# One product on constants ahead of the taps' product in a vision tower, and key weights issued by ScalarE

## The chip, the cores and the metric

The kernel runs on one core of a Trainium2 chip. TensorE multiplies matrices, VectorE, ScalarE and GpSimd do the rest, and SyncE (SP) issues most of the transfers between memory (HBM) and the core's SBUF. The number to compare is the device time of one execution in microseconds (us). Before the change it is 248.19 us, the median of 3 runs (247.21 to 248.34).

## The reference

Eight pictures of 3 x 256 x 256 go through an edge filter, one causal attention head, a layer norm, a mixture of 8 experts with a capacity, and a second layer norm.

```python
# x (8, 3, 256, 256); scharr (2, 1, 3, 3): the taps; D = 256, 8 experts, F = 1024
gray = einsum('bchw,c->bhw', x, (0.2989, 0.587, 0.114))
h = sum over both filters of |conv3x3(gray, scharr)| / 2          # (8, 256, 256): 256 tokens of 256
Q, K, V = h @ Wq.T + bq, h @ Wk.T + bk, h @ Wv.T + bv
h = layernorm(h + softmax(causal(Q @ K.T / 16)) @ V)
probs = softmax(h @ Wr);  idx = argmax(probs)                     # each token goes to one expert
kept = position within its expert < 320
ffn = where(kept, (relu(t @ W1[idx]) @ W2[idx]) * max(probs), t)
out = layernorm(h + ffn)
```

## The kernel before, in words

The program is written by engine: a block for each of SyncE, GpSimd, ScalarE, VectorE and TensorE, each run in the order in which it stands, with semaphores between them. There is no planner: the order is written out by hand. Most products are done in three parts on fp32r halves ("high" and "low" of a number), the setup products in fp32, which the trace shows as two passes each.

The stages are: a setup; then a loop over the 8 pictures, which interleaves the convolution of the next picture (`convolve`, as products with band matrices) with the attention of the present one; then a loop over 8 experts. TensorE goes from one to the next with hardly a break. The change touches the setup alone, the first 10 us:

- SyncE issues the taps (18 numbers), Wq, Wk, the top and the bottom half of the first picture, Wv, Wr, the second picture and the biases of the values (lines 369 to 380).
- VectorE sets `one_row` (a row of ones, line 917) and fills one quarter of `xT_hi` with ones (line 918; the trace calls this memory `w_hi`). Then it scales the spread taps (`half_taps`, 920) and builds the three bands (`make_band`, lines 900 and 908), with two parts of them from ScalarE, and then the first picture's gray values (927 to 934, the trace's `red`).
- ScalarE issues the key bias (749, into the last column of `wk`), copies the row of ones (752, which brings a table load), makes parts of the bands (758), issues the query bias (760), rounds the bands (636, `band_high`) and then the gray values (764, 766).
- TensorE spreads the taps over 128 partitions with a product of `one_row` and `taps` (1463). Behind it come six products on the ones (`keep_warm`, 1458), whose result no one reads; they fill the time in which the weights of the keys are under way. Then `setup_keys` multiplies Wq and Wk (1302; it waits for both, `attn_w_in` at 32, and for the key bias, `key_bias_in`), `setup_biases` makes the bias terms (1311, 1314; waits for the query bias), and the convolution of the first picture begins (1364; waits for the bands and the high half of the gray values, `first_gray_ready`).

Of the kernel before, what the change touches and what calls it, by code (L numbers as in the profile page):

```python
# [10 lines left out]
F32 = mybir.dt.float32  # L11
# [21 lines left out]
def vit_tower_kernel(  # L33
# [13 lines left out]
):  # L47
    B, CH, S, D = x.shape
    E, _, F = W1.shape
    DC, SC, FC = D // P, S // P, F // P  # L50
    T = B * S
# [15 lines left out]
    with ExitStack() as ctx:  # L67
        def sb(name, shape, dt=F32):
            return ctx.enter_context(nc.sbuf_tensor(name, shape, dt))

        def sem(name):
            return ctx.enter_context(nc.semaphore(name))
# [22 lines left out]
        wk = sb("wk", [P, DC, D + 1])  # L95
# [22 lines left out]
        def halves(start, *dims):  # L118
            n = int(np.prod(dims))
            names = "abc"[:len(dims)]  # L120
            cut = f"p ({' '.join(names)}) -> p {' '.join(names)}"
            sizes = dict(zip(names, dims))
            return [t[:, start:start + n].rearrange(cut, **sizes) for t in (attn_hi, attn_lo)]

        xT_hi, xT_lo = halves(0, 2, DC, S)
# [124 lines left out]
        attn_w_in = sem("attn_w_in")  # L250
        wv_in = sem("wv_in")
        still_ready = sem("still_ready")
# [80 lines left out]
        def _(sp):  # L333
# [34 lines left out]

            sp.dma_start(taps[:, :], bass.AP(scharr.tensor, 0, [[0, 1], [1, TAP_COLS]])).then_inc(taps_in, 16)
            sp.dma_start(wq[:, :, :], Wq.rearrange("(p c) d -> p c d", c=DC)).then_inc(attn_w_in, 16)  # L370
            sp.dma_start(wk[:, :, 0:D], Wk.rearrange("(p c) d -> p c d", c=DC)).then_inc(attn_w_in, 16)
            sp.dma_start(pix[:, 0, :, 0, :], x[0, :, 0:P, :].rearrange("c p d -> p c d")).then_inc(first_pix, 16)
            sp.dma_start(pix[:, 0, :, 1, :], x[0, :, P:S, :].rearrange("c p d -> p c d")).then_inc(pix_in[0], 16)
            sp.dma_start(wv[:, :, :], Wv.rearrange("(c p) d -> p c d", p=P)).then_inc(wv_in, 16)
# [247 lines left out]
        def _(act):  # L622
# [117 lines left out]
            def split_high(n):  # L740
# [4 lines left out]
                if e >= 2:  # L745
                    act.wait_ge(h_used, FC * (e - 1))
                act.activation(w_hi[:, e % 2, c], w_raw[:, e % 2, c], ACT.Copy).then_inc(w_hi_ready, 1)  # L747

            act.dma_start(wk[:, :, D:D + 1], bk.rearrange("(p c o) -> p c o", c=DC, o=1),
                          allow_slow_non_contiguous=True).then_inc(key_bias_in, 16)  # L750
            act.wait_ge(row_ready, 1)
# [82 lines left out]
            def norm_out(e):  # L834
                act.wait_ge(yrstd_ready, e + 1)
                if e >= 2:
                    act.wait_ge(z_out[e % 2], 16 * NS * (e // 2))
                for j, (_, n) in enumerate(SLOTS):
                    ins = act.activation(z[0:n, e % 2, j, :], y[0:n, e % 2, j, :], ACT.Identity,  # L839
                                         bias=ynmr[0:n, e % 2, j:j + 1], scale=yrstd[0:n, e % 2, j:j + 1])  # L840
                ins.then_inc(z_ready, 1)
# [22 lines left out]
        def _(dve):  # L864
# [6 lines left out]
            def settle():  # L871
                dve.wait_ge(dve_step, steps[0])
# [23 lines left out]
            def make_band(dx):  # L896
# [8 lines left out]
                for dy in range(1, TAPS):  # L905
# [8 lines left out]
                    if dy < TAPS - 1:  # L914
                        settle()

            dve.memset(one_row[:, :], 1.0).then_inc(row_ready, 1)
            dve.memset(xT_hi[:, 0].bitcast(F32), 1.0).then_inc(still_ready, 1)
            dve.wait_ge(taps_spread, 1)
            dve.tensor_scalar(half_taps[:, :], bank[4][:, 0:TAP_COLS], 0.5 * GRAY[0], None, ALU.mult).then_inc(scaled_ready, 1)  # L920
            dve.wait_ge(mask_ready, TAPS)
# [291 lines left out]
            def expert_out(e):  # L1213

                if e >= 2:
                    dve.wait_ge(z_ready, e - 1)
                dve.wait_ge(turned, e + 1)
                if e == 0:
                    dve.wait_ge(ein_in[0], 64)
                for j, (_, n) in enumerate(SLOTS):  # L1220
                    at, o = TURNED[j]
                    dve.scalar_tensor_tensor(y[0:n, e % 2, j, :], bank[at][0:n, o:o + D],
                                             ein[0:n, e, j, D:D + 1], ein[0:n, e, j, 0:D],
                                             ALU.mult, ALU.add).then_inc(y_ready, 1)

            def expert_stats(e):
                for j, (_, n) in enumerate(SLOTS):
                    dve.wait_ge(y_ready, NS * e + j + 1)
                    step(dve.bn_stats(ystats[0:n, j, :], y[0:n, e % 2, j, :]))
# [58 lines left out]
        def _(pe):  # L1288
# [8 lines left out]
            def setup_keys():  # L1297
                pe.wait_ge(attn_w_in, 16 * 2)
                pe.wait_ge(key_bias_in, 16)
                for c, to in enumerate((bank[3], bank[6])):  # L1300
                    for k in range(DC):
                        ins = pe.matmul(to[:, 0:D + 1], wq[:, k, c * P:(c + 1) * P],  # L1302
                                        wk[:, k, :], start=(k == 0), stop=(k == DC - 1))
                ins.then_inc(setup_mm, 1)
# [151 lines left out]
            def keep_warm(n):  # L1456
                for _ in range(n):
                    pe.matmul(bank[3][:, :], xT_hi[:, 0, 0, 0:P], xT_hi[:, 0].rearrange("p c s -> p (c s)"),  # L1458
                              start=True, stop=True)

            pe.wait_ge(row_ready, 1)
            pe.wait_ge(taps_in, 16)
            pe.matmul(bank[4][:, 0:TAP_COLS], one_row[:, :], taps[:, :], start=True, stop=True).then_inc(taps_spread, 1)
            pe.wait_ge(still_ready, 1)
            keep_warm(6)
            setup_keys()
            setup_biases()
            for s in range(SC):
# [58 lines left out]
            def early_turn():  # L1527
                pe.wait_ge(rowc_ready, B)
                pe.wait_ge(ein_in[0], 32)
                pe.wait_ge(spare_rows_ready, 1)  # L1530
                for c in range(DC):
                    for j, (o, _) in enumerate(SLOTS):
                        ins = pe.matmul(bank[c][:, o:o + P], ein[:, 0, j, c * P:(c + 1) * P], ident[:, :],
                                        start=(j == 0), stop=False, is_transpose=True, skip_group_check=True)
                ins.then_inc(early_turned, 1)
# [125 lines left out]
```

## Time and profile before

| | us |
|---|---|
| median of 3 runs | 248.19 (247.21 to 248.34) |
| the profiled execution | 248.55 |
| its span, first to last instruction | 246.7 |
| TensorE busy | 231.8 (94%) |
| VectorE busy | 185.3 (75%) |
| ScalarE busy | 152.1 (62%) |
| GpSimd busy | 99.4 (40%) |

The profile is of one execution. Its span leaves out 1.85 us that the time holds. Times in rows count from the start of the span. PE is TensorE's products, PEld its loading of weights, DVE VectorE, ACT ScalarE, POOL GpSimd; SPq and ACTq are the sequencers of SyncE and ScalarE when they issue transfers. The end of a product is modelled, since products overlap in the array: the step from one start to the next tells its rate better than its own duration does. L12 is line 12 of the kernel.

### The profile page before, as it was taken

To read this page: it belongs to the slowest core of one execution; us is meant where nothing else is said; L and a number is where in the kernel's file an instruction comes from. 1 tells how busy PE (TensorE), PEld (TensorE's weight loads), DVE (VectorE), ACT (ScalarE), POOL (GpSimd) and SP (SyncE) were. 2 spreads that over 40 slices of the span, in tenths; PEclk is the share of its full clock that TensorE was granted. 3 is DMA by queue.
4 is the path that set the end of the run, shared out by engine and by line. 5 is a ranking of instruction groups with operands and counts; after the bars stand their busy time and mean duration, and the time that the engine had idled before them with its cause. 6 is when DMAs were issued, how large, how long until landed. Compare 5 with 4: busy or idle time off the path is not lost.

```text
span 246.7 us, 4992 instructions
## 1 busy us (share of the span) xinstructions
PE 231.8 (94%) x1670; PEld 222.6 (90%) x1670; DVE 185.3 (75%) x559; ACT 152.1 (62%) x355; POOL 99.4 (40%) x169
## 2 busy tenths in 40 slices
PE   6999999999999999878999999999999999999940
PEld 4999999999999998656999999999999999999940
DVE  6868797888878798976666787867878678789550
ACT  5337567786877787465675676575765757666100
POOL 7000227484655669448100025133261322613672
PEclk9999999999999999999999999999999999999995
DMA  5925994174796020201799929156091550100100
GB/s 163 286 87 137 254 297 140 35 230 154 231 383 231 12 82 3 84 0 48 182 348 303 372 45 332 53 172 205 5 339 53 173 200 3 47 0 24 35 4 0
DMA packets 28379, 35.48 MB, mean 144 GB/s; under 512 B 2781, under 2 KB 25292, under 8 KB 28355
## 3 DMA queue, kind: packets, MB, share of 16 engines
q1 hardware_dynamic: 26146, 31.71, 40.8%
q0 software_dynamic: 1792, 3.47, 3.9%
q8 instruction: 13, 0.21, 0.4%
q14 instruction: 12, 0.09, 0.1%
q10 hardware_dynamic: 416, 0.00, 0.1%
HBM read 26.97 MB, written 9.47 MB: 148 GB/s over the span
## 4 chain that ended last, share of the span: by engine, by line
PE 82%; issue 5%; DVE 4%; POOL 4%; ACT 2%; POOLq 1%; DMA 0%; DVEq 0%; ACTq 0%
PE bank L1293 15%; PE bank L1294 15%; PE bank L1295 15%; PE bank L1364 12%; PE bank L1381 5%; PE bank L1418 4%; POOL out_dram L575 3%; PE bank L1547 2%; PE bank L1434 2%; PE bank L1597 2%; PE bank L1392 1%; PE bank L1302 1%; PE bank L1436 1%; PE bank L1435 1%; PE bank L1458 1%
## 5 line engine op out<-in xcount | busy, mean ns | idle before, releaser
L1210 DVE SCALAR_TENSOR_TENSOR h_lo<-bank,h_hi 128x320 fp32r<-128x320 f32 x58 | 28.4, 490 | 26.8 <-ACT h_hi L822 24.0
L822 ACT ACTIVATE h_hi<-bank 128x320 fp32r<-128x320 f32 x58 | 25.4, 438 | 36.8 <-PE bank L1295 36.8
L1293 PE MATMUL bank<-einT_hi,w_hi 128*128 128x320 f32 x128 | 40.4, 316 | 0.5 <-DVE einT_lo L1202 0.3
L1295 PE MATMUL bank<-einT_hi,w_lo 128*128 128x320 f32 x128 | 39.6, 309 | 0.0
L575 POOL DMA_INDIRECT out_dram<-tokens_mem,images x24 | 27.8, 1157 | 29.3 <-ACT tokens_mem L839 22.2
L1294 PE MATMUL bank<-einT_lo,w_hi 128*128 128x320 f32 x128 | 39.5, 309 | 0.0
L959 DVE TENSOR_TENSOR w_lo<-w_raw,w_hi 128x1024 fp32r<-128x1024 f32 x32 | 38.9, 1215 | 0.0
L1293 PE MATMUL bank<-h_hi,w_hi 128*128 128x320 f32 x112 | 35.2, 315 | 0.1
L1294 PE MATMUL bank<-h_lo,w_hi 128*128 128x320 f32 x112 | 34.6, 309 | 0.0
L1295 PE MATMUL bank<-h_hi,w_lo 128*128 128x320 f32 x112 | 34.6, 309 | 0.0
L747 ACT ACTIVATE w_hi<-w_raw 128x1024 fp32r<-128x1024 f32 x32 | 33.7, 1053 | 0.0
L569 POOL TENSOR_TENSOR yrstd<-yve,minus_half 128x3 f32<-128x3 f32 x6 | 5.3, 880 | 55.1 <-DVE yve L1241 55.1
L1293 PEld LDWEIGHTS bank<-einT_hi,w_hi 128*128 128x128 f32 x128 | 24.0, 188 | 1.6 <-issue 1.0
L1294 PEld LDWEIGHTS bank<-einT_lo,w_hi 128*128 128x128 f32 x128 | 24.1, 188 | 0.0
L1295 PEld LDWEIGHTS bank<-einT_hi,w_lo 128*128 128x128 f32 x128 | 24.0, 188 | 0.0
L1293 PEld LDWEIGHTS bank<-h_hi,w_hi 128*128 128x128 f32 x112 | 21.1, 188 | 0.3 <-issue 0.3
L1294 PEld LDWEIGHTS bank<-h_lo,w_hi 128*128 128x128 f32 x112 | 21.1, 188 | 0.0
L1295 PEld LDWEIGHTS bank<-h_hi,w_lo 128*128 128x128 f32 x112 | 21.0, 188 | 0.0
L525 POOL DMA_INDIRECT dispatched<-trow,slot x16 | 16.4, 1026 | 7.3 <-issue 5.7
L1364 PE MATMUL bank<-w_hi 128*128 128x260 f32 x96 | 15.1, 292 | 0.0
L1293 PE MATMUL bank<-w_hi 128*128 128x274 f32 (+2 forms) x50 | 14.5, 291 | 0.4 <-DVE w_lo L1210 0.4
L1364 PE MATMUL bank<-w_lo,w_hi 128*128 128x260 f32 x96 | 14.8, 291 | 0.0
(232 smaller groups left out, 575.4 us busy)
## 6 DMA issues: line engine op xcount, KB each, us to landing
w_raw<-in_L_ffn_W_dram SPq DMA_DIRECT2D x16, 1024.0 KB
images<-in_x_dram SPq DMA_DIRECT2D x7, 768.0 KB
dispatched<-blank SPq DMA_DIRECT2D x4, 645.0 KB, 10.0
images<-dispatched SPq DMA_DIRECT2D x9, 258.0 KB, 5.9
out_dram<-lone SPq DMA_DIRECT2D x8, 256.0 KB, 6.9
images<-in_x_dram SPq DMA_DIRECT2D x2, 384.0 KB, 4.5
images<-dispatched SPq DMA_DIRECT2D x9, 64.5 KB, 7.1
out_dram<-tokens_mem,images POOLq DMA_INDIRECT x24
```

The lines of the kernel that those rows point to most:

```text
L525: pool.indirect_dma_start(dispatched, bass.IndirectOffsetOnAxis(ap=slot[:, b % TR, s:s + 1], axis=0), trow[:, b % TR, s, :], None, bounds_ ...
L575: pool.indirect_dma_start(out_rows, bass.IndirectOffsetOnAxis(ap=ein[0:n, e, j, D + 1:D + 2].bitcast(U32), axis=0), z[0:n, e % 2, j, :], N ...
L747: act.activation(w_hi[:, e % 2, c], w_raw[:, e % 2, c], ACT.Copy).then_inc(w_hi_ready, 1)
L822: act.activation(hidden_halves(n)[0], bank[n % 2][:, 0:CAP], ACT.Relu).then_inc(h_hi_ready, 1)
L959: dve.tensor_tensor(w_lo[:, e % 2, c], w_raw[:, e % 2, c], w_hi[:, e % 2, c].bitcast(F32), ALU.subtract).then_inc(w_lo_ready, 1)
L1210: dve.scalar_tensor_tensor(lo, bank[n % 2][:, 0:CAP], 0.0, hi.bitcast(F32), ALU.max, ALU.subtract).then_inc(h_ready, 1)
L1293: pe.matmul(to, ah, bh, start=first, stop=False)
L1294: pe.matmul(to, ah, bl, start=False, stop=False)
L1295: return pe.matmul(to, al, bh, start=False, stop=last)
L1364: ins = pe.matmul(acc[:, :, s * (S - REACH):s * (S - REACH) + REACH], half[:, b % 2, s, c * P + dx:c * P + dx + P], of_band[:, dx, :, 2 - ...
L1381: ins = pe.matmul(bank[3][:, c * S:(c + 1) * S], half[:, k, c * P:(c + 1) * P], of_x[:, b % 2, k, :], start=(t == c == k == 0), stop=(t == ...
L1418: ins = pe.matmul(bank[6][:, s * S:s * S + n], half[:, k, s * P:(s + 1) * P], of_x[:, b % 2, k, 0:n], start=(t == s == k == 0), stop=(t == ...
```

## The change

TensorE does one of the products on constants before the product that spreads the taps, and five behind it. For that VectorE fills the ones first and sets the row of ones second. Wk is issued by ScalarE's queue, ahead of the key bias, and no longer by SyncE's.

```diff
@@ -368,7 +368,6 @@
             sp.dma_start(taps[:, :], bass.AP(scharr.tensor, 0, [[0, 1], [1, TAP_COLS]])).then_inc(taps_in, 16)
             sp.dma_start(wq[:, :, :], Wq.rearrange("(p c) d -> p c d", c=DC)).then_inc(attn_w_in, 16)
-            sp.dma_start(wk[:, :, 0:D], Wk.rearrange("(p c) d -> p c d", c=DC)).then_inc(attn_w_in, 16)
             sp.dma_start(pix[:, 0, :, 0, :], x[0, :, 0:P, :].rearrange("c p d -> p c d")).then_inc(first_pix, 16)
@@ -746,6 +745,7 @@
+            act.dma_start(wk[:, :, 0:D], Wk.rearrange("(p c) d -> p c d", c=DC)).then_inc(attn_w_in, 16)
             act.dma_start(wk[:, :, D:D + 1], bk.rearrange("(p c o) -> p c o", c=DC, o=1),
                           allow_slow_non_contiguous=True).then_inc(key_bias_in, 16)
             act.wait_ge(row_ready, 1)
@@ -914,8 +914,8 @@
+            dve.memset(xT_hi[:, 0].bitcast(F32), 1.0).then_inc(still_ready, 1)
             dve.memset(one_row[:, :], 1.0).then_inc(row_ready, 1)
-            dve.memset(xT_hi[:, 0].bitcast(F32), 1.0).then_inc(still_ready, 1)
             dve.wait_ge(taps_spread, 1)
@@ -1458,11 +1458,12 @@
+            pe.wait_ge(still_ready, 1)
+            keep_warm(1)
             pe.wait_ge(row_ready, 1)
             pe.wait_ge(taps_in, 16)
             pe.matmul(bank[4][:, 0:TAP_COLS], one_row[:, :], taps[:, :], start=True, stop=True).then_inc(taps_spread, 1)
-            pe.wait_ge(still_ready, 1)
-            keep_warm(6)
+            keep_warm(5)
             setup_keys()
```

TensorE's order at the start of the program, before and then after; `one_row` and `taps` are the taps' product, `w_hi` the ones:

```order
L1287 UNCONDITIONAL_BRANCH
L1463 MATMUL bank<-taps,one_row 128x18
L1458 MATMUL bank<-w_hi 128x512 x6
L1302 MATMUL bank<-wk,wq 128x257 x4
L1311 MATMUL bank<-bqc,wk 128x1 x4
L1314 MATMUL bank<-wk,bqc 128x1 x2
```

```order
L1287 UNCONDITIONAL_BRANCH
L1458 MATMUL bank<-w_hi 128x512
L1465 MATMUL bank<-taps,one_row 128x18
L1458 MATMUL bank<-w_hi 128x512 x5
L1302 MATMUL bank<-wk,wq 128x257 x4
L1311 MATMUL bank<-bqc,wk 128x1 x4
```

One of the six products stands ahead of the taps' product; the rest of TensorE's order is as it was.

SyncE's transfers at the start, the piece of the difference (- before, + after); `images` is the picture:

```order
 L369 DMA taps<-in_L_tok_scharr_dram 1x18
 L370 DMA wq<-in_L_attn_Wq_dram 128x512
-L371 DMA wk<-in_L_attn_Wk_dram 128x2x256
+L371 DMA images<-in_x_dram 128x3x256
 L372 DMA images<-in_x_dram 128x3x256
-L373 DMA images<-in_x_dram 128x3x256
-L374 DMA wv<-in_L_attn_Wv_dram 128x2x256
-L375 DMA wr<-in_L_ffn_Wr_dram 128x2x8
+L373 DMA wv<-in_L_attn_Wv_dram 128x2x256
+L374 DMA wr<-in_L_ffn_Wr_dram 128x2x8
```

Everything behind Wq moves up by one place in SyncE's queue. ScalarE's start, the other end of that move, after the change:

```order
L748 DMA wk<-in_L_attn_Wk_dram 128x2x256
L749 DMA wk<-in_L_attn_bk_dram 128x2x1
L752 ACT_TABLE_LOAD
L752 ACTIVATE still_row<-one_row 1x128
L758 ACTIVATE images<-images,half_taps 128x132 x4
L760 DMA bqc<-in_L_attn_bq_dram 128x2
```

Before, the same rows stood there without the first.

## Rows read from the trace of the kernel before

**Rows 1.** The page: shares of the chain that ended last, by engine

```profile
PE 82%; issue 5%; DVE 4%; POOL 4%; ACT 2%; POOLq 1%; DMA 0%; DVEq 0%; ACTq 0%
```

**Rows 2.** Waits of TensorE, whole span: total us, times, longest us

```profile
PE bank L1463 <- DMA taps<-in_L_tok_scharr_dram: 2.1, 1, 2.1
```

**Rows 3.** The chain in order of time: start us, us, what

```profile
0.80 1.21 DMA taps<-in_L_tok_scharr_dram
...
2.72 2.86 PE bank L1458 x6
```

**Rows 4.** TensorE, narrow stretches, and its weight load: start us, us, line, operation

```profile
2.65 0.80 PE L1458 MATMUL bank<-w_hi 128*128 128x512 f32 x1
...
4.95 0.63 PE L1458 MATMUL bank<-w_hi 128*128 128x512 f32 x1
5.38 0.76 PE L1302 MATMUL bank<-wk,wq 128*128 128x257 f32 x1
...
5.34 3.07 PEld L1302 LDWEIGHTS bank<-wk,wq 128*128 128x128 f32 x8 [0.48 <-DMA wk<-in_L_attn_Wk_dram]
...
8.07 0.60 PE L1302 MATMUL bank<-wk,wq 128*128 128x257 f32 x1
8.50 0.39 PE L1302 MATMUL bank<-wk,wq 128*128 128x257 f32 x1
8.72 0.28 PE L1311 MATMUL bank<-bqc,wk 128*128 128x1 f32 x2
```

**Rows 5.** Busy time by stretch; at the end granted clock, DMA share, GB/s

```profile
2.00:3.00 1.00, 0.86 (x3) 0.85 (x4) 0.18 (x1) 0.99 (x3) 0.80 (x9) 1.00 0.09 7
3.00:4.00 1.00, 1.00 (x3) 0.81 (x3) 0.92 (x4) 1.00 (x5) 0.94 (x5) 1.00 0.93 321
```

**Rows 6.** VectorE in order of time, 0 to 9 us

```profile
0.88 0.17 DVE L917 MEMSET one_row<- 1x128 f32 x1 [0.88 <-PEq L1648]
1.10 0.48 DVE L918 MEMSET w_hi<- 128x512 f32 x1
...
7.34 0.42 DVE L927 SCALAR_TENSOR_TENSOR red<-images 128x256 f32<-128x256 f32 x1
...
8.78 0.43 DVE L932 SCALAR_TENSOR_TENSOR red<-images 128x256 f32<-128x256 f32 x1 [0.56 <-DMA images<-in_x_dram]
```

**Rows 7.** Issues and ScalarE in order of time, 0 to 6 us

```profile
0.81 0.64 ACTq L749 DMA_DIRECT2D wk<-in_L_attn_bk_dram  x1
...
1.21 0.37 SPq L370 DMA_DIRECT2D wq<-in_L_attn_Wq_dram  x1
...
1.48 1.28 ACT L752 ACT_TABLE_LOAD   x1 [1.48 <-PEq L1648]
1.62 0.67 SPq L371 DMA_DIRECT2D wk<-in_L_attn_Wk_dram  x1
...
2.98 0.40 ACTq L760 DMA_DIRECT2D bqc<-in_L_attn_bq_dram  x1
2.99 1.28 ACT L758 ACTIVATE images<-images,half_taps 128x132 f32<-128x132 f32 x4
...
5.04 0.42 ACT L636 ACTIVATE w_hi<-images 128x264 fp32r<-128x264 f32 x1 [0.78 <-DVE images L908]
```

**Rows 8.** Transfers issued up to 24 us: KB each, median us to landing

```profile
wq<-in_L_attn_Wq_dram SPq DMA_DIRECT2D x1, 256.0 KB, 3.4
wk<-in_L_attn_Wk_dram SPq DMA_DIRECT2D x1, 256.0 KB, 3.7
...
wk<-in_L_attn_bk_dram ACTq DMA_DIRECT2D x1, 1.0 KB, 3.2
bqc<-in_L_attn_bq_dram ACTq DMA_DIRECT2D x1, 1.0 KB, 4.7
```

**Rows 9.** ScalarE's first gray values and TensorE's first convolution, in order of time

```profile
8.26 0.42 ACT L764 ACTIVATE w_hi<-red 128x256 fp32r<-128x256 f32 x1 [0.37 <-DVE red L929]
...
9.98 0.97 PE L1364 MATMUL bank<-w_hi 128*128 128x260 f32 x6
```

## The prediction

> **What bounds the kernel now.** I read the page's busy shares and its chain's shares first, to see whether the start of the program matters at all. TensorE is busy for 94% of the span (the table) and carries 82% of the chain that ended last [rows 1]. So time taken away ahead of TensorE's first useful product moves the whole program, unless something later waits for a thing that doesn't move with it. The list of TensorE's waits says that nothing of the kind is near: the longest of the whole span is 2.1 us, for the taps at the start [rows 2], and no other transfer stands in it.
>
> Then I read the chain in order of time. It begins with the taps' transfer, runs through the taps' product and the six products on constants [rows 3] and on into the key product; TensorE's own instructions follow.
>
> Third came TensorE's single products at the start [rows 4]. The reader is to see start-to-start times: the products on constants (512 columns) follow each other at 0.43 us, the passes of the key product (257 columns, two passes for each fp32 product) at 0.43 us too, up to the one at 8.07. The one that starts at 8.50 gives way after 0.22 us. The granted clock is printed as 1.00 in these stretches [rows 5], but 512 columns in 0.43 us are the level of 1.2 GHz, and half of the time for the same pass is that of 2.4 GHz. So in this execution the clock rises at 8.5 us, 5.85 us after the first product on constants began; up to there each microsecond of TensorE's time does half of what it does later. That is the price used below: **whatever only moves work inside the low stretch is worth half its length.**
>
> Last, what feeds this stretch: VectorE's rows [rows 6], the issues on the two queues [rows 7] and the time from an issue to landing [rows 8].
>
> **The change, part by part.**
>
> *The first product on constants goes ahead of the taps.* Its data is the memset of 0.48 us, now first on VectorE. VectorE is free at 0.88 [rows 6], so it is done at 1.36. With 0.1 us for the handover (an estimate: TensorE began at 2.14, 0.13 us after the 2.01 at which the taps' piece of the chain ends [rows 3]) the product starts near 1.47 and gives way 0.43 us later, near 1.9 to 2.0. TensorE sat idle there until 2.14. The taps' product is queued behind it: if the taps come at 2.14 as before, the margin is 0.15 us. Should it miss them, VectorE's scaling of the taps, the three bands and the picture's top rows at 7.34 are late by as much; I cost this at nothing, at most 0.2 us. The row of ones moves behind the long memset and is ready at about 1.53: ScalarE uses it only after its table load (ends 2.76), TensorE not before 2.14. Nothing is lost.
>
> *Five products in place of six behind the taps.* The first starts at 2.65 as before, the key product at 5.38 - 0.43 = 4.95. If the clock still rises at 8.50, the eight passes start from 4.95 to 8.07 and the next instruction (the bias product, at 8.72 before) at 8.50: **0.22 us gained**. Its lower end is 0, if the operands are not there at 4.95; no row makes the removed pass worth more than 0.43 us.
>
> *The clock.* TensorE now does its first wide product 1.18 us earlier (1.47 for 2.65), with a gap of about 0.2 us and the narrow taps' product behind it. Four executions of the same program took 247.21 to 248.55 us, a spread of 1.34 us, and the one with the profile is the slowest of them. At half a microsecond per microsecond of late rise, 1.34 us are 2.7 us of the clock's rise, so I read the rise at 8.50 as a late one, and the moment as not tied firmly to the program (an estimate from the spread; one trace can't show it). Then an earlier first product moves the rise by something between nothing (if the gap spoils what came before it) and the whole 1.18 us on average: 0 to 0.59 us of time. I take **0.35 us**, a bit over the middle, since the gap is short beside what is filled.
>
> The Trainium skill bears on that: "TensorE: Matmul & The Clock Gate", Part 1, What's actually happening, says that the chip's monitor of TensorE's activity runs freely and doesn't restart with the kernel, so that the moment of the rise varies between runs. The spread of the times agrees; that the rise moved in the other three executions no row shows.
>
> *Key weights from ScalarE's queue.* Before, Wk was issued at 1.62 as SP's third transfer and landed 3.7 us later, at 5.32; TensorE's weight load waited for it until 5.34 [rows 4]. It would be too late for the key product at 4.95. Now it goes out at 0.81, first on ScalarE's queue. With the same 3.7 us it lands at 4.51; Wq, issued at 1.21, at 4.61 as before [rows 7, 8]. The key bias is issued behind Wk's 0.67 us, at 1.48, and lands at 4.68 by its old 3.2 us. All three are in by 4.95, with 0.27 us to spare. The first ends of these are not sure: the bias ran at a time when the DMA engines were nearly idle (a share of 0.09 between 2 and 3 us), while from 3 us on the share is 0.93 and more [rows 5]. The query bias, a transfer of the same small kind sent at 2.98 into this traffic, took 4.7 us. With 4.7 us [rows 8] the key bias lands at 6.2. So the key product starts between 4.95 and 6.2; I take 4.95 to 5.1, as the bias still goes out before the traffic starts, and keep 6.2 for the range.
>
> ScalarE's engine waits behind one more issue: 0.67 us. Its table load moves from 1.48 to 2.15 and ends at 3.43, the copy of the row of ones at 3.7; its four band products start then in place of 2.99 and end near 5.0. ScalarE's next step waited for VectorE's first band until 5.04 [rows 7], and VectorE needs ScalarE's parts only behind that band. So it is hidden with some 0.05 us of cover. Without it the bands are late by the excess, up to 0.3 us, which stands against the slack ahead of the convolution, below.
>
> *SP's queue moves up by 0.7 us.* Picture, value weights and router weights are issued 0.7 us earlier, by Wk's issue of 0.67. VectorE had idled 0.56 us for the picture's second half at 8.78 [rows 6]; that wait goes. No one on TensorE's side gains by it now, but it is cover for a convolution that starts earlier: the first one, at 9.98, needs the high half of the picture's top rows, which ScalarE finishes at 8.26 + 0.42 = 8.68 [rows 9]. That comes from the band work on VectorE and doesn't move. So 1.3 us is the most that this part of the program can give, whatever the clock does.
>
> **The sum.** 0.22 + 0.35 = 0.57 us against the profiled execution's 248.55 (span 246.7, 1.85 us around it) would be 247.98. The median of the three timed runs stands 0.36 us under it, and a median is what I forecast: 248.19 - 0.57 = **247.6 us**. About 0.5%, 1.24 us, is what a measurement of this kernel can tell from no change.
>
> **The rivals.**
>
> *A rise one good step earlier.* If filling the time from 1.47 makes the clock rise before the key product is through, the gain isn't 0.35 us but the cap of 1.3: the key passes at 0.22 us would be done by about 7, the bias product would wait for the query bias (2.98 + 4.7 = 7.7), and the convolution would start at 8.7 for 9.98. That is 248.19 - 1.3 = 246.9. For it: the late rise in the profiled run leaves room. Against: the product ahead of the taps is short, and a gap follows it.
>
> *No effect.* The operands set the start of the key product at 5.4, or the rise stays where it was and the 0.22 us drown: 248.1. For it: Wk was the last to come by 0.02 us of 5.34, and the DMA engines are full from 3 us on.
>
> *Slower: the key operands share their DMA engines with the picture.* Before, the 384 KB of the picture's top half stood behind Wk in one queue. Now SP's queue holds Wq and then the picture, ScalarE's holds Wk and then the key bias, and both run at once. If they alternate, the last of Wk or its bias may come when all 896 KB are through: from 3.0 us on at 321 GB/s [rows 5] that is 5.8 us, and 0.7 us more for the landing (512 KB were through at 4.6 by this rate, and Wk landed at 5.32): 6.5 us. It decides from a landing later than 5.38, and each microsecond beyond costs 0.5 us: 0.55 us at 6.5, and TensorE's idle time of 1.5 us from 4.95 could put the clock's rise off by as much, another 0.75 us. That is 248.7 to 249.5; I take 249.0. Against it: Wk goes out 0.4 us ahead of Wq, and before it the engines are empty.
>
> The Trainium skill names this against the change: "DMA: Bandwidth & Descriptors", Issuing engines are not separate DMA queues, says that transfers of all issuing engines run on the same 16 DMA engines and interleave, and that a second issuer saves only the time to issue. By that rule the gain is the 0.81 us of the earlier issue and no bandwidth.
>
> *It doesn't do what it says.* If the memset or TensorE's start is later than 1.7, the product pushes the taps behind 2.14: the band chain and everything to 8.68 slip by 0.2 to 0.3 us, still under the 1.3 us of slack. That ends as no effect.
>
> **How the numbers follow.** Forecast 0.55, rise a step earlier 0.18, no effect 0.17, slower by the shared engines 0.10. The timed runs of one program spread over 1.1 us, so a median can be off by 0.5 us either way. The likeliest case spans 247.0 to 248.2. With the cap case (246.9, less the scatter) and the mild half of the slow one the range is 246.5 to 248.8. Faster by over 0.5% (under 246.95) takes most of the cap case and a tail of the forecast: 0.22. Slower by over 0.5% (over 249.43) is the upper end of the slow case: 0.05. The rest, 0.73, is within 0.5%.
>
> **What would show it.** A product on constants at about 1.47, the taps' product still at 2.14, the key product at 4.95 with no wait for Wk or its bias; the start from which passes take 0.22 us, earlier or at 8.50; the convolution's first product at 9.76 or earlier. Wrong: TensorE idle ahead of the key product, a taps' product after 2.2, ScalarE's bands ending after 5.1, or a convolution that starts at 9.98 or later.

## The result: slower by 0.5%, and a third of the executions by much more

| | before | after |
|---|---|---|
| median, us (19 runs each) | 248.10 | 249.27 |
| lowest to highest | 247.21 to 248.50 | 248.17 to 253.91 |
| executions over 251 us | 0 | 7 |
| ratio, with 95% interval | | 1.0052 (1.0033 to 1.0071) |
| the profiled execution, and its span | 248.55, 246.7 | 251.67, 249.9 |

The ratio leaves out the executions more than 1.5% above the lowest of their kernel, here the five of 252.5 us and more; what went on in such executions is told below. The twelve under 250 have a median of 248.76, still 0.7 us above the kernel before. Of the kernel before none of the 70 runs beside the experiments was over 249 us.

The page of the changed kernel, two rows of its 40 equal slices (6.25 us each): TensorE's busy share and the granted clock, in tenths.

```profile
PE   7899999999999999978999999999999999999940
...
PEclk9769999999999999999999999999999999999996
```

TensorE is as busy as before, but in the second and third slice it was granted 7 and 6 tenths of its full clock (2.4 GHz). TensorE in order of time after the change:

```profile
1.51 0.80 PE L1458 MATMUL bank<-w_hi 128*128 128x512 f32 x1 [1.51 <-DVE w_hi L917]
2.23 0.61 PE L1465 MATMUL bank<-taps,one_row 1*128 1x18 f32 x2
2.77 2.50 PE L1458 MATMUL bank<-w_hi 128*128 128x512 f32 x5
5.23 2.60 PE L1302 MATMUL bank<-wk,wq 128*128 128x257 f32 x8
8.81 1.05 PE L1311 MATMUL bank<-bqc,wk 128*128 128x1 f32 x8 [0.98 <-DMA bqc<-in_L_attn_bq_dram]
...
10.41 1.65 PE L1364 MATMUL bank<-w_hi 128*128 128x260 f32 x6
```

The early product is there, at 1.51 against the 1.47 forecast. The eight key passes start at 5.23 and are through at 7.83, where before they ran from 5.38 to the product at 8.72 [rows 4]: the clock rose early. The single passes show where; the starts of two that follow each other, 0.43 us apart up to 6.22, are at 6.58 and 6.80:

```profile
6.58 0.60 PE L1302 MATMUL bank<-wk,wq 128*128 128x257 f32 x2
6.80 0.60 PE L1302 MATMUL bank<-wk,wq 128*128 128x257 f32 x2
```

So the rise came near 6.5, where [rows 4] had it at 8.50. And then TensorE waits 0.98 us for the query bias, and some 1.1 us after that wait the clock falls. The stretches (length, busy time of PE, PEld, DVE, ACT, POOL, then granted clock, DMA share, GB/s):

```profile
7.00:8.00 1.00, 0.83 (x4) 0.38 (x2) 0.97 (x4) 0.42 (x1) 0.00 (x0) 1.00 1.14 337
8.00:9.00 1.00, 0.19 (x2) 0.19 (x2) 0.97 (x3) 0.42 (x1) 0.00 (x0) 1.00 1.10 357
9.00:10.00 1.00, 1.00 (x11) 1.00 (x10) 0.45 (x2) 0.42 (x1) 0.00 (x0) 0.96 1.11 340
10.00:11.00 1.00, 1.00 (x6) 1.00 (x7) 1.00 (x2) 0.00 (x0) 0.00 (x0) 0.50 1.10 233
...
16.00:18.00 2.00, 2.00 (x15) 2.00 (x15) 0.00 (x0) 0.00 (x0) 0.00 (x0) 0.81 0.00 0
```

A granted 0.96 of the stretch from 9 to 10 puts the fall at 9.92, 0.81 of that from 16 to 18 puts the return at 16.76. That is 6.8 us at 1.2 GHz, in which TensorE is never idle; at half price they would cost 3.4 us. Product by product, the last key pass starts 1.04 us ahead of where it was before (7.46 for 8.50), the bias product 0.09 us behind (8.81 for 8.72), and by 16.8 TensorE is 3.3 us behind: the early rise is eaten by the wait, and the fall costs 3.2 us. The first convolution product starts at 10.41 in place of 9.98 [rows 9]; its six products take 1.65 us in place of 0.97. The spans differ by 3.2 us. The last product starts 3.2 us later too, so nothing further on adds to it on the whole.

The chain of the changed kernel, start us, us, what:

```profile
0.79 0.65 ACTq L748
...
1.47 0.64 ACTq L749
...
2.23 1.20 issue
...
3.44 5.33 DMA bqc<-in_L_attn_bq_dram
8.77 0.04 issue
8.81 1.05 PE bank L1311 x8
```

The chain doesn't begin with the taps any more. It runs over ScalarE's two issues and its table load to the query bias, issued at 3.44, and on to TensorE. The transfers, median us to landing, which answer to [rows 8]:

```profile
wk<-in_L_attn_Wk_dram ACTq DMA_DIRECT2D x1, 256.0 KB, 3.6
wq<-in_L_attn_Wq_dram SPq DMA_DIRECT2D x1, 256.0 KB, 3.7
...
wk<-in_L_attn_bk_dram ACTq DMA_DIRECT2D x1, 1.0 KB, 3.6
bqc<-in_L_attn_bq_dram ACTq DMA_DIRECT2D x1, 1.0 KB, 5.3
```

### The profile page after: what moved, and what is told of

It reads as the page before. It is cut to its first block, busy times and chain, and to the rows that moved or that the text cites. A ratio compares the mean times of both kernels' runs of the same rounds, so it can differ in the third digit from the quotient of the medians.

```text
span 249.9 us, 4992 instructions
## 1 busy us (share of the span) xinstructions
PE 234.7 (94%) x1670; PEld 225.1 (90%) x1670; DVE 184.9 (74%) x559; ACT 152.1 (61%) x355; POOL 98.6 (39%) x169
## 4 chain that ended last, share of the span: by engine, by line
PE 81%; issue 4%; POOL 4%; DVE 4%; ACT 2%; DMA 2%; POOLq 1%; ACTq 1%; DVEq 0%
PE bank L1293 15%; PE bank L1295 15%; PE bank L1294 15%; PE bank L1364 14%; PE bank L1381 5%; PE bank L1418 4%; POOL out_dram L574 3%; DMA bqc<-in_L_attn_bq_dram 2%; PE bank L1548 2%; PE bank L1434 2%; PE bank L1598 2%; PE bank L1392 1%; PE bank L1436 1%; PE bank L1435 1%; POOL yrstd L598 1%
## 5 line engine op out<-in xcount | busy, mean ns | idle before, releaser
L1364 PE MATMUL bank<-w_hi 128*128 128x260 f32 x96 | 16.4, 311 | 0.0
L947 DVE TENSOR_TENSOR xT<-tokens_mem 128x256 f32<-128x256 f32 x16 | 8.3, 522 | 10.3 <-ACT tokens_mem L642 10.3
L642 ACT ACTIVATE tokens_mem<-bank 128x512 f32<-128x512 f32 x16 | 9.6, 598 | 10.0 <-PE bank L1364 9.9
## 6 DMA issues: line engine op xcount, KB each, us to landing
dispatched<-blank SPq DMA_DIRECT2D x4, 645.0 KB, 10.2
```

Source lines behind the costliest of these rows:

```text
L1364: ins = pe.matmul(acc[:, :, s * (S - REACH):s * (S - REACH) + REACH], half[:, b % 2, s, c * P + dx:c * P + dx + P], of_band[:, dx, :, 2 - ...
```

## The experiments

Two theories go through the expectations. The *gap theory*: TensorE has to wait for a late query bias behind an early rise of the clock, and the wait makes the clock fall. The *order theory*: the early product by itself brings the early rise and the fall.

**One part of the change at a time.** The first kernel has the early product and leaves Wk in SyncE's queue; the second moves Wk and leaves the products alone; the third is the changed kernel with the query bias moved.

```diff
 e1, against after
+            sp.dma_start(wk[:, :, 0:D], ...)     # behind wq
-            act.dma_start(wk[:, :, 0:D], ...)
 e2, against before
-            sp.dma_start(wk[:, :, 0:D], ...)
+            act.dma_start(wk[:, :, 0:D], ...)    # ahead of the key bias
 e3, against after
+            sp.dma_start(bqc[:, :], ...)         # behind wq
-            act.dma_start(bqc[:, :], ...)
```

> The order of the change alone: one product on constants ahead of the taps' product and five behind it, Wk still on SyncE's queue, so that the query bias is issued at 2.98 and lands near 7.7 again. Gap theory (TensorE starves for the query bias behind an early rise of the clock, and the clock falls back): the wait for the query bias is at most 0.3 us, no fall, or a rare one; 247.5 to 248.1 us. Order theory (the early product by itself brings the early rise and the fall, whatever the queue does): as slow as the changed kernel, 249.3 us, with executions over 251.

Measured: 248.28 us, ratio 1.0012 (1.0000 to 1.0024), none of 12 over 248.7. The order theory falls. So does the forecast of a gain. In TensorE's order of time of e1 the first convolution product starts 0.17 us earlier than before, and the last product of the program (the start at 237.06 before) 0.03 us:

```profile
9.81 0.99 PE L1364 MATMUL bank<-w_hi 128*128 128x260 f32 x6
...
237.03 0.28 PE L1295 MATMUL bank<-w_hi,w_lo 128*64 128x256 f32 x1
```

> The queue move alone: Wk issued by ScalarE's queue ahead of the key bias, taps' product first, six products on constants behind it. Query bias lands near 8.8. Gap theory: the rise comes as late as before in most executions, so the late query bias is mostly hidden behind the key product's slow passes (8.72): 248.1 to 248.8 us, with executions over 251 only where the rise comes early. Order theory: 248.1, none over 251. A theory that the queue alone does the harm: 249.3 us as the changed kernel.

Measured: 248.96 us, ratio 1.0050 (1.0024 to 1.0077), 3 of 12 over 251 (252.10, 253.80, 254.19). Wk's place alone does the harm, executions over 251 with it, and without any early product. TensorE's key product in e2:

```profile
5.88 3.40 PE L1302 MATMUL bank<-wk,wq 128*128 128x257 f32 x8 [0.31 <-DMA wk<-in_L_attn_bk_dram]
```

This is a wait that I hadn't in this theory: for the key bias, which lands 4.3 us after its issue at 1.47.

> The changed kernel with the query bias issued by SyncE right behind Wq (at about 1.6 us) in place of ScalarE's queue at 3.44. It should land before 7 us, so that the bias products follow the key product at once. Gap theory: no idle time at 7.7 to 8.8, no fall of the clock, 247.2 to 247.9 us. Order theory: still a fall in a third of the executions, since products of one column are light work whether late or not: 249 us.

Measured: 248.29 us, ratio 1.0012 (1.0001 to 1.0023), none of 12 over 248.8. The executions over 251 are gone and nearly all of the loss with them, but the gain of 247.2 to 247.9 isn't there. (In e3 the key bias came early enough too, in at 5.09, and e14 and e15 below are alike, so e3 may take away both waits and not only the one for the query bias.)

**Filling the wait.** Five more products on constants between the key product and the bias products, into another bank:

```diff
             setup_keys()
+            keep_warm(5, bank[7])
             setup_biases()
```

> The changed kernel with five more products on constants (bank 7) between the key product and the bias products, about 1.1 us at the high clock: TensorE isn't idle while the query bias is under way. Gap theory: the clock doesn't fall; executions over 251 us are gone, and the others stay at 248.3 to 249, since the wait is only filled: median 248.6. Order theory or another cause of the fall: executions over 251 stay.

Measured: 249.63 us, ratio 1.0075 (1.0054 to 1.0096), none of 6 over 250.7. No execution over 251, as expected, though six are few where 7 of 19 had been over it; and slower than expected. In its profile the key product started at 5.51 and the clock rose near 7.9, and the five products, from 8.29 on, were work in front of a query bias that had landed at 8.44 (3.44 + 5.0).

**The late query bias alone**, in the kernel before:

```diff
+            band_high(0)
             act.dma_start(bqc[:, :], ...)
-            for dx in range(TAPS):
+            for dx in range(1, TAPS):
                 band_high(dx)
```

> The kernel before, with the query bias alone issued later: behind ScalarE's first rounding of a band, at about 5.1 in place of 2.98. It lands near 10, so that TensorE has nothing to do for 0.8 to 1.5 us ahead of the bias products. Nothing else of the change is in. Gap theory (a wait for the query bias ahead of the bias products makes the clock fall back or rise much later): executions over 251 us in a third or more, and the others about 1 us slower than before: 249 us or more. If Wk's place or the early product makes the dear executions: 249 us, none over 251.

Measured: 254.0 us, ratio 1.0217 (1.0189 to 1.0246), all of 4 over 252.6. TensorE's bias product in e5, and then stretches of TensorE alone:

```profile
10.88 1.86 PE L1312 MATMUL bank<-bqc,wk 128*128 128x1 f32 x8 [3.13 <-DMA bqc<-in_L_attn_bq_dram]
```

```profile
8.00:9.00 1.00, 0.00 (x0) 1.00 1.08 360
9.00:10.00 1.00, 0.00 (x0) 0.87 1.13 329
...
19.00:20.00 1.00, 1.00 (x6) 0.51 0.00 0
20.00:21.00 1.00, 1.00 (x10) 1.00 0.00 0
```

(PE alone: length, busy time, granted clock, DMA share, GB/s.) A wait of 3.13 us behind an early rise, the fall at 9.7 inside it, and the return only near 20. Wk is in its old place here and there is no early product: a wait at this place is enough.

**The query bias early**, with the early product (e6, on top of e1) and without (e7, on top of before):

```diff
             act.dma_start(wk[:, :, D:D + 1], bk...)
+            act.dma_start(bqc[:, :], ...)
             ...
-            act.dma_start(bqc[:, :], ...)     # behind the band parts
```

> The early product and Wk on SyncE's queue, with the query bias issued by ScalarE right behind the key bias (at 1.45 in place of 3.10). It lands before 6. If the wait for the query bias is what hides the gain of an early rise of the clock, executions with an early rise now gain: 247.0 to 247.6 us. If the early product has nothing to give: as the order alone, 248.0 to 248.3.

> The kernel before with the query bias issued by ScalarE right behind the key bias, nothing else. In the profiled execution of before the query bias was in 1.0 us ahead of its use, so no effect where the clock rises late: 247.9 us. Where it rises early, TensorE would have waited a little; gap theory gives up to 0.5 us in these: 247.5 to 247.9.

Measured: e6 248.33 us, ratio 1.0006 (0.9994 to 1.0019); e7 248.14 us, ratio 1.0003 (0.9987 to 1.0019). No version beats the kernel before. Both profiles caught an early rise (near 6.5 and 6.4 by the steps), with the same products of one column behind it and no wait ahead of them (e7's wait of 0.49 us, below, comes behind them), and neither shows a fall. So in these two an early rise and narrow products alone didn't bring the fall; the wait is what the first profile and e5 have in addition. e6 shows what an early rise is worth:

```profile
7.59 0.95 PE L1311 MATMUL bank<-bqc,wk 128*128 128x1 f32 x8
...
8.85 0.98 PE L1364 MATMUL bank<-w_hi 128*128 128x260 f32 x6
...
236.66 0.28 PE L1295 MATMUL bank<-w_hi,w_lo 128*64 128x256 f32 x1
```

The bias product is 1.13 us earlier than before and the convolution 1.13, but the last product of the program 0.40. The traces, laid side by side, show where the lead goes: at the wait of 0.18 us for Wv its product starts at 10.01 for 10.79, a lead of 0.78; the lead is 0.54 by 84 us, and behind a wait for VectorE that grows from 0.36 to 0.52 us (230.35 for 230.75) it is 0.4. e7 waits for the gray values:

```profile
9.49 1.02 PE L1364 MATMUL bank<-w_hi 128*128 128x260 f32 x6 [0.49 <-ACT w_hi L764]
```

This is the cap of the prediction, and here it leaves 0.49 us and not 1.3: the picture came late, VectorE waited 0.69 us for it and began the gray values at 8.10 for 7.34, and ScalarE had the high half at 9.44 for 8.68.

**More profiles of the changed kernel** (e8 to e11, the same code):

> The changed kernel once more, for one profile: a second look at when the clock rises. Gap theory: either a fall behind the wait of about 1 us for the query bias, as in the first profile, or, if the rise comes after 8.5, no fall and no wait, and about 248.5 us.

> The changed kernel again, for one profile. Some of its executions took over 253 us, with a recorded clock of 0.99 and so no recorded fall. Gap theory: in those the clock's first rise comes only after 13 us, since the wait for the query bias lies where the first rise would have been decided; TensorE's products would then step at the low level (0.22 us for 260 columns) from the start to there. If such an execution is caught, a fall behind an early rise, or anything late in the program, would contradict this. Otherwise 248.5 to 249.5 us with a rise near 9.

> The changed kernel again. An execution over 253 us shows a first rise after 13 us (gap theory), one of 251 to 252.5 a rise before 7.7 and a fall near 10, one under 250 a rise between 8 and 10 and no fall.

> The changed kernel once more. Gap theory gives the same three cases: over 253 us with a first rise after 13 us; 251 to 252.5 with an early rise and a fall near 10; under 250 with a rise between 8 and 10.

Measured: 249.11, 249.01, 249.46 and 253.77 us. The first three end alike, by two ways. In e8 the key product starts at 5.18, but its last pass (8.31) is followed by the bias product only at 9.07, when the query bias has landed (3.44 + 5.6); in e9 and e10 the key product starts at 5.92 and 6.24, behind a wait of 0.65 and 0.96 us for the key bias. The clock is up near 9, and the convolution starts at 10.44 to 10.72, 0.5 to 0.7 us later than in [rows 9]. The fourth is of another kind. TensorE in order of time in e11:

```profile
5.94 3.77 PE L1302 MATMUL bank<-wk,wq 128*128 128x257 f32 x8 [0.67 <-DMA wk<-in_L_attn_bk_dram]
9.50 1.71 PE L1311 MATMUL bank<-bqc,wk 128*128 128x1 f32 x8
...
11.92 1.65 PE L1364 MATMUL bank<-w_hi 128*128 128x260 f32 x6
...
16.38 2.68 PE L1364 MATMUL bank<-w_hi,w_lo 128*128 128x260 f32 x12
18.89 1.65 PE L1364 MATMUL bank<-w_lo,w_hi 128*128 128x260 f32 x12
20.38 0.95 PE L1337 MATMUL bank<-side,wv 128*128 128x8 f32 x8
```

Six convolution products in 1.65 us and twelve in 2.5 are the low level, from the start to about 18.8; the next twelve run at 0.12 us each. So here the clock never fell, it first rose at 18.8, and the last product of the program starts 5.3 us later than before (242.35 for 237.06). As in the stretches of before, the printed clock is 1.00 until then and doesn't tell it; the steps do. The wait ahead of it is the one for the key bias (landed 4.3 us after its issue), not the one for the query bias as I had it. The mean granted clocks of the seven executions over 251 in the result fall into the same two kinds: 0.976 to 0.978 in three (251.36 to 252.54 us), as in the profile with the fall, and 0.990 to 0.991 in four (252.85 to 253.91 us), as in e11.

**Which of the two waits.** e12 issues the key bias ahead of Wk, e13 both biases ahead of Wk; e14 and e15 are e3's code.

```diff
 e12, against after (e13 moves the bqc line up with it)
-            act.dma_start(wk[:, :, 0:D], ...)
             act.dma_start(wk[:, :, D:D + 1], bk...)
+            act.dma_start(wk[:, :, 0:D], ...)
```

> The changed kernel with the key bias issued ahead of Wk on ScalarE's queue. The key bias lands near 3.7 as in the kernel before, Wk (issued at 1.47) near 5.1; the query bias stays late, near 8.8. Theory that the key bias's wait makes the slow executions: none over 251, 248.0 to 248.4 us. Theory that the query bias's wait alone is enough: still some of 251 to 254, those with an early rise, and the rest near 248.4.

Measured: 249.11 us, ratio 1.0043 (1.0021 to 1.0066), 1 of 12 over 251 (252.06, with a mean granted clock of 0.977 like the first profile of the changed kernel), none over 253. The key bias is in after 3.0 us, and yet the loss stays. TensorE's weight loads in e12:

```profile
5.38 3.07 PEld L1302 LDWEIGHTS bank<-wk,wq 128*128 128x128 f32 x8 [0.83 <-DMA wk<-in_L_attn_Wk_dram]
8.71 0.61 PEld L1311 LDWEIGHTS bank<-bqc,wk 128*128 128x128 f32 x2 [0.25 <-DMA bqc<-in_L_attn_bq_dram]
```

By its clock one execution in twelve fell. The profile doesn't show that the query bias costs the rest: it had landed at 8.64, and the bias product at 8.97 follows the last key pass (8.54) by the 0.43 us of a low pass. The product is 0.25 us later than before because the clock rose near 9.4 here, and not at 8.50. That a query bias at 8.6 takes away what executions with an earlier rise would gain is argued. The other kind, of 252.8 us and more with a mean clock of 0.99, 4 of 19 in the changed kernel, didn't come in 12: that fits the key bias, and isn't proof.

> The changed kernel with both biases issued ahead of Wk on ScalarE's queue: key bias lands near 3.7, query bias near 4.4, Wk (issued at about 1.9) near 5.4. Either theory: none over 251. Key product at 5.4 in place of 5.2 at worst: 247.8 to 248.4 us, no different from the kernel before.

Measured: 254.35 us, ratio 1.0204 (1.0153 to 1.0255). A plain miss: Wk, issued at 2.13, takes 5.8 us to land. Between 4 and 5 us ScalarE's queue moved 0.01 MB and SyncE's 0.37 MB; Wk's bytes moved almost all between 5 and 6 us, and of its sixteen steps the last but one came at 6.55 and the last at 7.91.

```profile
7.95 3.79 PE L1302 MATMUL bank<-wk,wq 128*128 128x257 f32 x8 [2.67 <-DMA wk<-in_L_attn_Wk_dram]
```

The miss answers the question all the same. Both biases are in by 4.9, TensorE waits once, ahead of the key product, and not ahead of the bias products (11.54, right behind the last key pass). The clock first rises near 20.5, and five of the six executions have the mean clock of 0.99 and take 254.3 us or more; none has the clock of a fall. So a wait ahead of the key product alone, here for Wk, makes the kind with the late first rise, as the wait ahead of the bias products in e5 makes the kind with the fall (0.971 to 0.981 in all four).

> The changed kernel with the query bias on SyncE's queue behind Wq, one more profile of the same kernel as e3. If the query bias's place was what made the key bias late, the key bias lands within 3.7 us of its issue and TensorE doesn't wait for it. If not, it lands up to 4.6 us after its issue here too, with a wait of 0.2 to 1 us ahead of the key product.

> The same kernel as in the look before, once more, with the same two possibilities: key bias within 3.7 us of its issue and no wait, or up to 4.6 us and a wait ahead of the key product.

Measured: 248.37 and 248.61 us; the key bias lands after 3.8 and 3.6 us, the key product starts at 5.38 and 5.18. The profile names Wq as what ended the idle time of the weight load, but the two weights were in by 4.97 and 4.87 and the key bias at 5.25 and 5.04: it is the key bias that the start follows, by 0.13 us, here as in all ten profiles with Wk ahead of it. What differs is how late it is, and in the late ones that is often the last of the sixteen steps in which a transfer counts up its semaphore: in e10 the fifteenth came at 5.11 and the last at 6.10, in e11 at 5.29 and 5.81, in e2 at 5.16 and 5.75. So in three profiles with the query bias on SyncE's queue (e3, e14, e15) the key bias took 3.6 to 3.8 us; in the seven with it on ScalarE's queue (the changed kernel five times, e2, e4) 3.6 to 4.6. The ranges overlap, and why the last step is late in some executions isn't shown.

## Why the prediction was wrong

The direction was wrong: 247.6 was forecast, 249.27 measured, outside 246.5 to 248.8. By its steps:

*First product and five behind it.* The mechanism was right. The product starts at 1.51, the taps' product at 2.23 where it had been at 2.14 (why it is 0.09 us late I didn't follow), and e1 shows 0.17 us at the convolution for the 0.22 forecast. The mistake is to carry that to the end of the program: of e1's 0.17 us the last product shows 0.03, of e6's 1.13 it shows 0.40. The prediction had read from [rows 2] that nothing later waits for a thing that doesn't move along; e6's wait for Wv, e7's for the gray values and the wait for VectorE at 230 are such things, and each takes a part.

*The clock.* The term of 0.35 us isn't there. e1 and before have the same time, and the profiles' rises scatter in both: near 8.5 before and 6.4 in e7 without the early product, 8.4 in e1 and 6.5 in e6 with it. That the moment isn't tied firmly to the program was right, and so was the price of half: in e7 the rise comes 2.1 us earlier and the last key pass starts 1.11 us earlier. That the early product moves the rise on average is not seen in the times.

*Key weights from ScalarE's queue* is the step that failed. Wk and Wq were both in by 4.94, in time for 4.95, against the 4.61 forecast. (They count on one semaphore, so that the landing given for each alone is only taken in the order of issue.) But the biases were costed by their old times. The key bias was taken at 3.2 us from issue to landing; behind Wk, in the traffic, it took 3.6 to 4.6 (the prediction had seen that this could be, and kept 6.2 as the latest start), and the key product started at 5.18 to 6.24 in place of 4.95, each time 0.13 us after the key bias. For the query bias I counted no delay at all ("2.98 + 4.7 = 7.7", in a rival): I had moved ScalarE's table load by the 0.67 us of the new issue and hidden it behind VectorE's bands, and forgot that the query bias's issue stands in the same order behind it. It moved to 3.44 and took 5.3 us: 8.77, against the 8.72 at which it had been used. The cover of 1.0 us that [rows 4, 7, 8] show for it was never written down as a cover.

*The rival that came true* is the one given 0.10: late key operands, from 5.38 on at half a microsecond each, and the clock's rise put off. Its place was right, its size wrong by the part that matters: I took a rise late by as much as TensorE's idle time (1.5 us, priced at 0.75); the rise at 18.8 in e11 is 10 us late behind a wait of 0.67 us, and the fall in the first profile costs 3.2 us behind one of 0.98. A fall of the clock stood in no rival. That the rival's 249.0 us is near the 249.27 measured is in part luck: its operands came at 6.5, and the wait for the query bias isn't in it. The rule of the Trainium skill that I set beside it ("DMA: Bandwidth & Descriptors", Issuing engines are not separate DMA queues) agrees with the traces: with Wk ahead of the key bias on ScalarE's queue both weights were in by 4.72 to 4.99 (ten profiles), with Wk behind Wq in SyncE's queue by 4.99 to 5.29 (five), some 0.2 us for an issue 0.8 us earlier, and the key bias took more.

*Shown and argued.* Shown by e1, e2 and e3: the loss comes with Wk's move, not with the early product, and goes when the query bias is taken off ScalarE's queue. Shown by e5: a wait ahead of the bias products is enough for the fall, and by e6 and e7: without the wait an early rise isn't followed by one. Shown by e13: a wait of 2.67 us ahead of the key product is enough for the late first rise. Argued from e11 and from e12's twelve executions without one: that the key bias's wait of 0.7 us does this in the changed kernel, where waits of 0.65 and 0.96 us (e9, e10) didn't. Open: what decides, from one execution to the next, whether the rise comes near 6.5, near 9, or at 18.8; why the last step of the key bias lands late in some; and which of the two waits makes most of the loss in the executions under 250.

## What to carry to other kernels

When a transfer is put ahead in a queue, list everything that its engine issues later, small loads included, and give each its new landing against its use; a 1 KB load that was 1 us early is cover that the move spends. A wait of TensorE in the first microseconds is not priced by its length: look at several executions, since in this program the clock turned waits of 0.98 and 0.67 us into 3.2 and 5.3 us in some of them. A median gain of 0.2 us at the start of a program is not yet a gain at its end.

## What the runs showed that I had not expected

- In the first profile of the changed kernel a fall came behind a wait of only 0.98 us: at 9.92, 1.1 us after TensorE had taken up work again, with products of one column. The clock came back 6.8 us later, with TensorE busy throughout; in e5, behind a wait of 3.13 us, after 10.2 us.
- The key bias, 1 KB in 4-byte pieces, took 2.8 to 3.2 us as the first transfer of its queue (seven profiles), and 3.6 to 4.6 behind Wk's 256 KB (ten). Wq and Wk together were in by 4.7 to 5.4 us when Wk was issued between 0.8 and 1.6, and by 7.9 when it was issued at 2.13 behind both biases (one profile, e13).
- The printed granted clock says 1.00 ahead of the first rise, where the products step at 1.2 GHz: 0.43 us for 512 columns, up to 18.8 us in one execution.
